# A recommender's interaction tower in float32: 14 instead of 12 second-layer tiles as split products, with a share of the splitting on GpSimd

## What is computed

```python
def _cin_layer(h, h0, W, b):
    Wr = W.reshape(W.shape[0], Hn, Mn)
    x = jnp.einsum('bhd,bmd,ohm->bod', h, h0, Wr) + b[None, :, None]
    return jax.nn.relu(x)
e = jnp.stack([tbl_0[ids[:, 0]], ..., tbl_31[ids[:, 31]]], axis=1)   # 1024 x 32 x 64
x1 = _cin_layer(e, e, W1, b1)                      # 128 outputs
direct2 = _cin_layer(x1[:, :64], e, W2, b2)        # 128 outputs, contraction over 64*32
z = jnp.sum(jnp.concatenate([x1[:, 64:], direct2], axis=1), axis=-1)
h = jnp.concatenate([z, dense_ctx], axis=1)
h = relu(h @ W_top1 + b_top1); h = relu(h @ W_top2 + b_top2); y = h @ W_top3
```

## Time and profile before

| | |
|---|---|
| median of 3 runs | 2056.95 us (2056.09 to 2058.79) |
| the profiled execution | 2060.19 us |
| its span | 2058.4 us |
| TensorE busy | 2016.3 us, 98% |
| VectorE busy | 1990.2 us, 97% |
| ScalarE busy | 1632.1 us, 79% |
| GpSimd busy | 1236.3 us, 60% |

### The profile page before, as it was taken

The page is one execution under the profiler, slowest core; times in us unless marked ns, Lnnn a source line. Parts: engine busy times, 40 slices in busy tenths (PEclk is TensorE's granted clock), DMA queues, the critical chain, the costliest instruction groups (busy, mean ns, idle before and its releaser), DMA issues.

```text
span 2058.4 us, 28705 instructions
## 1 busy us (share of the span) xinstructions
PE 2016.3 (98%) x6890; PEld 1300.9 (63%) x6890; DVE 1990.2 (97%) x545; ACT 1632.1 (79%) x4755; POOL 1236.3 (60%) x580
## 2 busy tenths in 40 slices
PE   3899999999999999999999999999999999999999
PEld 1566666666666666666666666666666666666664
DVE  5999999999999999999999999999999999999992
ACT  2688788788788788788888887887887887888873
POOL 3766666666765765665765766666666656666420
PEclk9899999999999999999999999999999999999999
DMA  5777677677677776776776776776776776767740
GB/s 185 206 208 212 197 208 214 193 210 211 196 202 215 198 213 202 199 215 199 204 214 197 207 216 194 205 219 187 216 211 193 211 208 197 214 203 203 212 108 1
DMA packets 239331, 406.51 MB, mean 197 GB/s; under 512 B 33377, under 2 KB 50273, under 8 KB 239090
## 3 DMA queue, kind: packets, MB, share of 16 engines
q1 hardware_dynamic: 231026, 397.10, 66.2%
q0 software_dynamic: 8192, 8.40, 2.3%
HBM read 321.49 MB, written 16.78 MB: 164 GB/s over the span
## 4 chain that ended last, share of the span: by engine, by line
DVE 58%; issue 36%; PE 3%; DMA 1%; SPq 1%; ACT 0%; POOL 0%; DVEq 0%; ACTq 0%; POOLq 0%
DVE pnear L455 25%; DVE plo L460 17%; DVE pfar L455 16%; PE acc L517 1%; ACT phi L651 0%; PE acc L523 0%; PE acc L534 0%; PE acc L582 0%; PE x1p L582 0%; PE acc L524 0%; POOL gathered L237 0%; DMA near<-emb_rows 0%; DMA rem_b<-emb_rows 0%; SPq L297 0%; PE acc L588 0%
## 5 line engine op out<-in xcount | busy, mean ns | idle before, releaser
L257 POOL TENSOR_TENSOR prod<-near,h 128x2048 f32<-128x2048 f32 x126 | 577.1, 4580 | 589.1 <-PE acc L518 585.9
L651 ACT CAST phi<-pnear 128x4096 fp32r<-128x4096 f32 x128 | 465.9, 3640 | 292.8 <-DVE pnear L455 292.7
L523 PE MATMUL acc<-phi,w2lo 128*128 128x512 f32 x1536 | 604.2, 393 | 12.4 <-ACT phi L651 12.4
L524 PE MATMUL acc<-phi,w2hi 128*128 128x512 f32 x1536 | 603.6, 393 | 0.0
L460 DVE TENSOR_TENSOR plo<-pnear,phi 128x4096 fp32r<-128x4096 f32 x128 | 586.6, 4583 | 1.7 <-ACT phi L651 1.7
L598 ACT ACTIVATE acc<-acc,bias 128x64 f32<-128x64 f32 (+1 forms) x2048 | 575.6, 284 | 11.8 <-PE acc L524 8.5
L455 DVE TENSOR_TENSOR pnear<-near,x1p 128x4096 f32<-128x4096 f32 x128 | 564.0, 4406 | 4.6 <-ACT x1p L634 4.6
L455 DVE TENSOR_TENSOR pfar<-far,x1p 128x4096 f32<-128x4096 f32 x128 | 564.1, 4407 | 3.0 <-PE acc L534 2.8
L237 POOL DMA_INDIRECT gathered<-in_tables,idx x256 | 473.5, 1850 | 104.3 <-POOL idx L232 51.9
L517 PE MATMUL acc<-prod,w1T 128*128 128x512 f32 x1024 | 466.1, 598 | 14.9 <-DVE prod L440 12.9
L534 PE MATMUL acc<-pfar,w2T 128*128 128x512 f32 x1024 | 460.4, 592 | 0.0
(11 more groups left out here) (68 smaller groups left out, 487.5 us busy)
## 6 DMA issues: line engine op xcount, KB each, us to landing
near<-emb_rows SPq DMA_DIRECT2D x512, 256.0 KB, 3.8
far<-emb_rows SPq DMA_DIRECT2D x512, 256.0 KB, 4.4
x1rep<-x SPq DMA_DIRECT2D x256, 256.0 KB, 4.1
h<-emb_rows SPq DMA_DIRECT2D x128, 256.0 KB, 3.1
emb_rows<-gathered SPq DMA_DIRECT2D x128, 128.0 KB, 3.5
gathered<-in_tables,idx POOLq DMA_INDIRECT x256, 3.9
rem_a<-emb_rows SPq DMA_DIRECT2D x64, 64.0 KB
rem_b<-emb_rows SPq DMA_DIRECT2D x64, 64.0 KB
```

The lines of the kernel that those rows point to most:

```text
L257: nc.gpsimd.tensor_tensor(prod1[:, :, :], near[(u + 2) % 3][:, :, :], h0[odd][:, :].unsqueeze(1).to_broadcast([P, K1, N]), ALU.mult).then_ ...
L523: nc.tensor.matmul(acc2[s][:, :], w2lo[:, t, :], phi[:, t, :], start=(t == 0), stop=False)
L524: mm = nc.tensor.matmul(acc2[s][:, :], w2hi[:, t, :], phi[:, t, :], start=False, stop=(t == T_SPLIT - 1))
L651: nc.scalar.copy(phi[:, 0:T_NEAR, :], pnear[:, :, :, :].rearrange("p a k n -> p (a k) n")).then_inc(hi_near_ready, 1)
```

## The change

14 tiles are split in place of 12. The two new ones are the first two of the far tiles' second half. ScalarE casts them together with the four far ones before them, in one instruction of 3072 elements a partition. VectorE's operations stay as they were; the low parts of the two new tiles are made by GpSimd, in one subtraction of 1024 elements a partition (`low` in its `step`). It stands first in the step of the following chunk and is followed by `idx`, `prod1` and the remainder; `rem_prod` moves from the start of the even step to the odd step, behind `prod1`. The lookups are last. TensorE now has 2 whole tiles, takes the far high products before the far low products, and ends a chunk with the low products of the two new tiles. Semaphores are split accordingly: VectorE's next `pfar` and ScalarE's next far cast wait for `lo_pool_ready`.

```diff
-T_SPLIT = T_NEAR + K2
+T_LOW = T_NEAR + K2
+T_SPLIT = T_LOW + 2
+T_WHOLE = T_NEAR + A2 * K2 - T_SPLIT
...
+            def remainder_products(pair):
+                pool.wait_ge(rem_in, 32 * pair + 32)
+
+                pool.wait_ge(rem_lo_ready, pair)
+                nc.gpsimd.tensor_tensor(rem_prod[:, :], rem_a[:, :], rem_b[:, :], ALU.mult).then_inc(rem_prod_ready, 1)
+
+            def low(c):
+
+                pool.wait_ge(lo_far_ready, c)
+                pool.wait_ge(hi_far_ready, c)
...
+                nc.gpsimd.tensor_tensor(plo[:, T_LOW:T_SPLIT, :], pfar[:, 1, 0:T_SPLIT - T_LOW, :],
+                                        phi[:, T_LOW:T_SPLIT, :].bitcast(fp32), ALU.subtract).then_inc(lo_pool_ready, 1)
...
                 if begun(at):
                     dve.wait_ge(lo_far_ready, c)
+                    dve.wait_ge(lo_pool_ready, c)
                     dve.wait_ge(far_used, c)
                 products2(pfar[:, :, :, :], far[odd][:, :, :], odd, K2).then_inc(pfar_ready, 1)
...
                 pe.wait_ge(lo_near_ready, c + 1)
-                low(odd, range(0, T_NEAR))
+                low(odd, range(0, T_NEAR)).then_inc(lo_near_used, 1)
+                pe.wait_ge(hi_far_ready, c + 1)
+                high(odd, range(T_NEAR, T_SPLIT)).then_inc(hi_far_used, 1)
                 pe.wait_ge(lo_far_ready, c + 1)
-                low(odd, range(T_NEAR, T_SPLIT)).then_inc(lo_used, 1)
-                pe.wait_ge(hi_far_ready, c + 1)
-                high(odd, range(T_NEAR, T_SPLIT)).then_inc(acc2_ready, 1)
+                low(odd, range(T_NEAR, T_LOW)).then_inc(lo_far_used, 1)
+                pe.wait_ge(lo_pool_ready, c + 1)
+                low(odd, range(T_LOW, T_SPLIT)).then_inc(acc2_ready, 1)
...
                 act.wait_ge(pfar_ready, c + 1)
                 if begun(at):
-                    act.wait_ge(acc2_ready, c)
-                nc.scalar.copy(phi[:, T_NEAR:T_SPLIT, :], pfar[:, 0, :, :]).then_inc(hi_far_ready, 1)
+                    act.wait_ge(hi_far_used, c)
+                    act.wait_ge(lo_pool_ready, c)
+                nc.scalar.copy(phi[:, T_NEAR:T_SPLIT, :], pfar[:, :, :, :].rearrange("p a k n -> p (a k) n")[:, 0:T_SPLIT - T_NEAR, :]
+                               ).then_inc(hi_far_ready, 1)
```

More of the change, by code:

```diff
@@ L247, in step @@
                 pair, odd = turn * (U // 2) + u // 2, u % 2
[L248 to L252, removed]
+                if begun(at):
+                    low(c)
+                if not odd and within(at, 7):
+                    pool.wait_ge(emb_stored, STORES * pair + STORES)
+                    place_idx(pair + 3, u // 2)
                 if within(at, 2):
@@ L259, in step @@
                                             ).then_inc(p1_ready, 1)
+                if odd and within(at, 3):
+                    remainder_products(pair + 2)
                 if not odd and within(at, 2):
@@ L268, in step @@
                     if not odd:
[L270 to L271 removed]
+                        pool.wait_ge(idx_ready, pair + 4)
+                        pool.sem_inc(lookups_begun, 1)
                     for g in range(2 * odd, 2 * odd + 2):
                         gather(g, u // 2)
+            remainder_products(1)
             software_pipeline(pool, step)
+            low(CHUNKS)
         @block.sync
@@ L422, in _ @@
             nc.vector.tensor_copy(flat(w1remT[:, :, :]), tp[1][0:3 * REM, 0:2 * P]).then_inc(tp_copied, 1)
[L423 to L430, removed]
+            for n, tiles in enumerate((range(T_LOW, T_SPLIT), range(0, K1), range(K1, T_NEAR), range(T_NEAR, T_LOW))):
+                hi, lo = (flat(w[:, tiles.start:tiles.stop, :]) for w in (w2hi, w2lo))
+                turned = tp[n % 2][:, 0:len(tiles) * O]
+                dve.wait_ge(tp_filled, 3 + n)
+                if n == 0:
+                    nc.vector.tensor_copy(flat(w2T[:, :, :]), tp[0][:, len(tiles) * O:K2 * O])
+                nc.vector.tensor_copy(hi, turned).then_inc(part_hi, 1)
+                dve.wait_ge(part_hi, n + 1)
+                nc.vector.tensor_tensor(lo, turned, hi.bitcast(fp32), ALU.subtract).then_inc(tp_copied, 1)
             dve.wait_ge(top_zero, 1)
@@ L476, in step @@
                 if begun(at):
-                    dve.wait_ge(lo_used, c)
+                    dve.wait_ge(lo_near_used, c)
                 low(slice(0, T_NEAR), pnear[:, :, :, :]).then_inc(lo_near_ready, 1)
                 dve.wait_ge(hi_far_ready, c + 1)
-                low(slice(T_NEAR, T_SPLIT), pfar[:, 0:1, :, :]).then_inc(lo_far_ready, 1)
+                if begun(at):
+                    dve.wait_ge(lo_far_used, c)
+                low(slice(T_NEAR, T_LOW), pfar[:, 0:1, :, :]).then_inc(lo_far_ready, 1)
             software_pipeline(dve, step)
@@ L528, in low @@
                 for t in parts:
-                    mm = nc.tensor.matmul(acc2[s][:, :], w2hi[:, t, :], plo[:, t, :], start=False, stop=False)
+                    mm = nc.tensor.matmul(acc2[s][:, :], w2hi[:, t, :], plo[:, t, :], start=False, stop=(t == T_SPLIT - 1))
                 return mm
             def whole(s):
-                for k in range(K2):
-                    mm = nc.tensor.matmul(acc2[s][:, :], w2T[:, k, :], pfar[:, 1, k, :], start=False, stop=False)
+                for t in range(T_WHOLE):
+                    mm = nc.tensor.matmul(acc2[s][:, :], w2T[:, t, :], pfar[:, 1, K2 - T_WHOLE + t, :], start=False, stop=False)
                 return mm
```

17 lines of the change are left out of this document (12 added, 5 removed).

## The result

The changed kernel takes 2264.86 us (median of 6 runs, 2263.15 to 2266.22) where the kernel before takes 2056.52: a ratio of 1.1005, 95% interval 1.0994 to 1.1016. It is 10% slower. The forecast was 2121.5 with a range up to 2160, so the time lies outside it. The rival that I had priced at 2232 us and given 0.13, the late remainder, is what happened, with one more stall on top.

The account below looks back on a forecast made before the run. TensorE bounds at 15.35 us a chunk, VectorE next at 15.20. GpSimd holding `plo` +65.1, last six chunks -1.0, last TensorE work -0.35, start +0.7: sum +64.5; 2060.2 + 64.5 - 3.2 = 2121.5 us, range 2040 to 2160.

Parts of the forecast that it names:

- the late remainder: GpSimd's `rem_parts` starts after near `plo`, is held, delays the far one 1.06 us; 16.8 a chunk, 2232 us; chance 0.13.
- What bounds the kernel before: TensorE leads with 15.35 us a chunk; VectorE needs 15.20 and is held back every second chunk by GpSimd.
- TensorE's and ScalarE's costs: TensorE saves 0.35 us, needing 15.0 a chunk; ScalarE's far cast grows 0.86 to 2.77, covered by idle time.
- GpSimd's chain: GpSimd's order, with a 2.39 us low part, pushes against VectorE's near `plo`: 15.90 us a chunk in place of 15.36.
- The three kinds of mutual exclusion: GpSimd work under way delays `plo`; GpSimd operations starting during `plo` are held until it ends; lookups are held likewise.
- the 0.12 that I took off an overlap: VectorE's `plo` is delayed by its overlap with running GpSimd work less 0.12 us: 0.57 odd, 0.84 even chunks.
- That rival (0.15): Lookups not held by far `plo`, or not at all; low part starts at +0.15 us; 2042.7 us; chance 0.15.
- The escaping lookup (0.10): Only the odd chunk's first lookup escapes being held by `plo`; 15.53 us a chunk, 2077 us; chance 0.10.
- so the low part starts not at +0.1, but at +0.9, always: GpSimd's low part starts 0.9 us after `pnear`, because held lookups end at +0.90 of the next chunk; main case, 0.62.
- the start is in that state before: Evidence for the 2232 us rival: near the kernel's start, `rem_parts` is already held and far `plo` takes 3.34 us.
- a margin of only 0.34 us in the loop: Time left for GpSimd's `rem_parts`, in even chunks, to start before VectorE's near `plo` at +8.66 us.

Follow-up runs that it names:

- the early load: SyncE's queue changed: looked-up rows stored earlier, the remainder's load one chunk earlier; as the only edit to the changed kernel with 14 tiles, 2105.72 us.
- the one wait at the start: Changed kernel with VectorE waiting for GpSimd's low part ahead of `pnear` in chunks 4 and 5 only: 2113.14 us.
- the whole tiles first: Changed kernel with TensorE's two whole tiles ahead of layer 1 in place of behind it: 2162.56 us.

## Why the prediction was wrong

**What bounds the kernel before** was right. TensorE's 15.35 and VectorE's 15.20 show in two experiments each: 15.35 with 12 tiles whatever the order, 15.20 with 13 tiles or without lookups, both with the early load.

**TensorE's and ScalarE's costs** were not contradicted. The far cast measured 2.78 us (2.77 worked out). TensorE's 15.0 us a chunk was never the bound in a run; what shows is that 14 tiles need no more than 15.20 at full clock.

**GpSimd's chain** held as to durations: the low part took 2.39 us on average, as taken. The three kinds of mutual exclusion, and the 0.12 that I took off an overlap, came back in the experiments: with the one wait at the start an overlap of 0.74 cost 0.62, one of 0.55 cost 0.43. The Trainium skill, "SBUF — State Buffer", section "Who interferes with whom", infers that a `tensor_tensor` does not stall the writing of DMA descriptors; in the kernel with the one wait at the start the lookups took 4.29 to 4.99 and 1.83 to 1.86 us instead of about 1, so here they are held, whatever the mechanism. That rival (0.15) is out: the lookup behind the far `plo` is held too. The escaping lookup (0.10) did not show either; the odd chunk's first lookup took 4.99.

**The step that failed** is "so the low part starts not at +0.1, but at +0.9, always". In the changed kernel it starts at +2.2 or later in every chunk from 1 to 122, and the far `plo`, which I had left at 2.28, takes 3.34. I worked out a state in which the chain closes on itself and took it for the only one. It exists (2113 us, against my 2121.5), but a second one closes on itself as well. I even wrote that "the start is in that state before", with the rows for it, and still gave it 0.13. It had already begun; what was owed was a reason why it should end. With a margin of only 0.34 us in the loop, the start had to be followed through chunk 1 as closely as the loop.

**Two terms were missing.** The move of `rem_prod` from the even to the odd chunk takes it nearer to its load. SyncE issues `rem_a` and `rem_b` in the same odd chunk, behind the copies of x1, and `rem_prod` waits for that load. With 13 tiles the wait of 1.06 us makes it run into the near `plo`, in the change one of 1.10 puts it behind the start of the near `plo`. I listed what the low part makes late, but not what the moved operation itself waits for. And TensorE's wait for `rem_parts`, which I had not put into the late-remainder case, stops it for 2.3 to 2.7 us; in 60 of 61 even chunks its clock is halved for a while behind it, and that comes back to VectorE as a wait for the whole tiles: 0.25 us a chunk. Without it the rival's price was right: 16.81 in chunk 55, 16.82 with the whole tiles first, against the 16.8 that I gave it (its own terms add up to 1.66, or 16.86). With the halved clock it became 17.07.

## What to carry to other kernels

When two engines exclude each other and one operation's start decides who is held, look for every order of events that repeats itself, and follow the first chunks to see into which one the kernel falls. A margin of a few tenths of a microsecond on a closed chain does not tell which state it will be. Of an operation that is moved, check first what it waits for at its new place. And work that is handed to an idle engine is free only in the part of the chunk in which that engine can run: GpSimd is 60% busy here, yet with the lookups a second tile did not fit ahead of the near `plo`.

## What the runs showed of the hardware

A GpSimd operation that is held by one VectorE subtraction goes first when that one ends, even if the next subtraction follows at once (the far `plo` at 3.34 to 3.38 us in place of 2.28), and a held lookup doesn't delay it (2.28). The shown start does not tell who won a tie: at 72.70 and 72.71 us of the changed kernel VectorE ran and GpSimd stood; at 511.20 and 511.21 with the whole tiles first it was the other way round. TensorE after a wait of 2.7 us for the remainder had a granted clock of 0.51 for 3.5 us, then 1.00 again. The wait alone does not bring this about: after one of 2.30 us (chunk 54 of the changed kernel) and after three of 2.67 to 2.80 us (early load) the clock stayed at 1.00. With the whole tiles ahead of layer 1 its idle time was 33 us in 383, and the clock stayed at 1.00, with the remainder still held. Two programs that differ by two waits before the loop ran 152 us apart.
